# Edge stage of a two-layer graph network: ScalarE seeds the accumulators and takes the second LayerNorm's squares, attributes scaled before they are turned, GpSimd's DMAs in pairs

## The reference

```python
h = max(layernorm(x), 0)
m = concat(h[dst], h[src]) @ W_pre.T + b_pre            # one message per edge
mx, mn, s1, s2 = segment max, min, sum of m, sum of m*m  by dst      # deg = edges per node
std = sqrt(relu(s2/deg - (s1/deg)**2) + 1e-5)
agg = concat(mx, mn, s1/deg, std)                       # 0 for mx, mn, mean without an edge
scaled = concat(agg, agg * log(deg+1), agg / log(deg+1))
x = x + (concat(h, scaled) @ W_post.T + b_post) @ W_lin.T + b_lin
h = max(layernorm(x), 0)
a = segment_sum(edge_attr, dst) / max(deg, 1)
x = x + relu(concat(h, a) @ W1 + b1) @ W2 + b2
```

## Time and profile before

| what | value |
|---|---|
| median of 3 runs | 1627.22 us (1627.15 to 1629.86) |
| profiled execution | 1626.46 us, its span 1624.7 us |
| granted TensorE clock, mean | 0.973 of full |
| PE, DVE, ACT, POOL busy | 92%, 86%, 58%, 76% |
| DMA moved | 197.95 MB |

### The profile page before, as it was taken

The page is one execution under the profiler, slowest core; times in us unless marked ns, Lnnn a source line. Parts: engine busy times, 40 slices in busy tenths (PEclk is TensorE's granted clock), DMA queues, the critical chain, the costliest instruction groups (busy, mean ns, idle before and its releaser), DMA issues.

```text
span 1624.7 us, 33700 instructions
## 1 busy us (share of the span) xinstructions
PE 1494.9 (92%) x8747; PEld 1257.4 (77%) x8747; DVE 1397.1 (86%) x4327; ACT 939.8 (58%) x1976; POOL 1236.0 (76%) x1376
## 2 busy tenths in 40 slices
PE   2899999999999759999999999999998999999995
PEld 2799998889999648888777787777777777777783
DVE  5899999999999468899888997988887888888892
ACT  1799999999999534455444453434444444444341
POOL 1778777777778777888888888888888888888833
PEclk9899999999999979999999999999999999999997
DMA  3455555555555622233233333333332323333200
GB/s 88 163 209 206 207 207 201 201 201 204 204 203 206 187 87 85 84 86 90 90 91 92 93 92 91 92 91 89 93 91 79 95 86 89 94 93 93 89 18 15
DMA packets 158898, 197.95 MB, mean 122 GB/s; under 512 B 18912, under 2 KB 115321, under 8 KB 158858
## 3 DMA queue, kind: packets, MB, share of 16 engines
q1 hardware_dynamic: 136906, 149.93, 28.3%
q0 software_dynamic: 21952, 47.55, 9.5%
HBM read 111.11 MB, written 90.17 MB: 124 GB/s over the span
## 4 chain that ended last, share of the span: by engine, by line
PE 82%; DVE 6%; issue 5%; ACT 3%; another core or an unknown queue 3%; DMA 1%; SPq 1%; POOL 0%; DVEq 0%; ACTq 0%; POOLq 0%
PE bank L572 12%; PE bank L621 6%; PE bank L581 6%; PE bank L614 5%; PE bank L691 5%; PE bank L618 5%; PE bank L615 5%; PE bank L624 5%; PE bank L704 5%; PE bank L670 3%; PE bank L593 3%; PE bank L591 3%; PE bank L592 3%; PE bank L555 3%
## 5 line engine op out<-in xcount | busy, mean ns | idle before, releaser
L444 POOL DMA_INDIRECT rows<-table,idx x196 | 208.3, 1063 | 59.7 <-issue 59.7
L450 POOL DMA_INDIRECT y<-nout,oidx x196 | 200.0, 1020 | 70.6 <-issue 70.3
L444 POOL DMA_INDIRECT hs<-table,idx x196 | 204.8, 1045 | 44.7 <-issue 31.2
L614 PE MATMUL bank<-comb_lo,agg_hi 128*128 128x384 f32 x588 | 212.4, 361 | 16.6 <-DVE nout L1019 10.7
L572 PE MATMUL bank<-w_sb,nut 128*128 128x128 f32 x1568 | 202.9, 283 | 5.5 <-issue 4.7
L379 POOL TENSOR_TENSOR runs<-nx,b_all 128x512 f32<-128x512 f32 x98 | 125.9, 1284 | 107.9 <-DVE nx L1029 107.8
L572 PEld LDWEIGHTS bank<-w_sb,nut 128*128 128x128 f32 x1568 | 184.5, 193 | 23.1 <-issue 14.2
L618 PE MATMUL bank<-comb_hi,agg_lo 128*128 128x384 f32 x588 | 200.1, 340 | 0.0
L615 PE MATMUL bank<-comb_hi,agg_hi 128*128 128x384 f32 x588 | 199.5, 339 | 0.0
L781 ACT ACTIVATE nh<-nx,nms,nrs 128x128 f32<-128x128 f32 x392 | 161.8, 484 | 1.1 <-DVE nms L1002 0.5
L621 PE MATMUL bank<-comb_sd,agg_sd 128*128 128x384 f32 x392 | 159.6, 489 | 0.0
(11 more groups left out here) (180 smaller groups left out, 4196.9 us busy)
## 6 DMA issues: line engine op xcount, KB each, us to landing
table<-rows SPq DMA_DIRECT2D x98, 512.0 KB, 2.7
rows<-in_x SPq DMA_DIRECT2D x98, 256.0 KB, 3.1
y<-nout SPq DMA_DIRECT2D x98, 256.0 KB
inv<-inv_row SPq DMA_DIRECT2D x49, 256.0 KB
attr<-in_edge_attr SPq DMA_DIRECT2D x48, 256.0 KB
keep<-keep_row SPq DMA_DIRECT2D x49, 128.0 KB
reset<-reset_row SPq DMA_DIRECT2D x49, 128.0 KB
lift<-lift_row SPq DMA_DIRECT2D x49, 128.0 KB
```

What stands on the lines that cost most here:

```text
L444: pool.indirect_dma_start(out=to[:, s, j, :], out_offset=None, in_=of, in_offset=bass.IndirectOffsetOnAxis(ap=idx[:, s, which, j:j + 1], a ...
L450: pool.indirect_dma_start(out=out, out_offset=bass.IndirectOffsetOnAxis(ap=oidx[:, c % 4, j:j + 1], axis=0), in_=eout[:, c % 2, j, :], in_ ...
L614: pe.matmul(acc[:, 0:SCALERS * P], hi, w_lo, start=(a == MX), stop=False, skip_group_check=True)
```

## The change

It touches the edge stage and what is prepared for it.

- *Accumulators.* `layer0` no longer begins a sum; ScalarE writes the constant part (b_post, b_lin and now b_pre through the weights, `acc_seed`, 128x384) into the bank first (`seed`, in place of PE's wait for mix), and the matmuls add to it. Two matmuls `open_sums` come once. With b_pre there, `message` goes: the scans read PE's bank, 3 and 4 in turn, and mix takes `xd` as gathered, so `receiver_const` goes too.
- *b2* is written into bank 7 by ScalarE (`out_bias`) and not by a matmul.
- *Second LayerNorm.* The last mix operation gives the row sum (`accum_out`), DVE makes the negative mean from it, ScalarE the sum of squares with four ACTIVATEs (`squares`).
- *Attributes.* ScalarE multiplies each attribute row by 1/count before it is turned (`scale_attr`), and the scan's mask becomes `keepm` = (count-1)/count in F32, a fifth mask row of 256 KB per chunk; `run_attr` is the mean itself, and `mean_attr` goes.
- *GpSimd* gathers three chunks ahead and not four, with `pause` between pairs of DMAs; three factors are copied, two chunks ahead.
- *Orders* of PE, ScalarE and DVE within a step are new.

```diff
@@ GpSimd @@
-            def mean_attr(c, i):
-                ...
-                pool.tensor_tensor(attr_mean[:, c % 2, :], run_attr[:, c % 2, :], inv[:, c % 4, :],
-                                   ALU.mult).then_inc(sem("e_attr_mean"), 1)
+            def pause(n, c, i):
+                pool.tensor_tensor(pause_go[:, n:n + 1], eps_col[:], eps_col[:], ALU.add).then_inc(sem(f"e_paused{n}"), 1)
+                pool.wait_ge(sem(f"e_paused{n}"), c + 1 + EU * i)
+                go(3 + n)
...
             def edge_step(k, i):
-                if edge(k + 1):
-                    copy_scales(k + 1, i)
...
+                if edge(k + 3):
+                    gather_rows_of(k + 3, i)
...
-                if edge(k):
-                    mean_attr(k, i)
...
@@ PE @@
             def layer0(c, j, i):
-                if j >= 2:
-                    pe.wait_ge(sem("e_mixed"), TILES * c + j - 1 + TILES * EU * i)
-                elif c >= 1:
-                    pe.wait_ge(sem("e_mixed"), TILES * (c - 1) + j + 3 + TILES * EU * i)
+                pe.wait_ge(sem("e_seeded"), TILES * c + j + 1 + TILES * EU * i)
...
             def outputs(c, i):
-                pe.matmul(bank[7][:], ones[:], b2_rows[:], start=True, stop=False, skip_group_check=True)
+                pe.wait_ge(sem("e_b2"), c + 1 + EU * i)
...
@@ ScalarE @@
+            def squares(c, i):
+                ...
+                for j in range(TILES):
+                    last = act.activation(off2[:, j, :], x1[:, b, j, :], ACT.Square, bias=neg2[:, b, j:j + 1],
+                                          accum_out=sq2[:, b, j:j + 1])
...
-            def message(c, i):
-                ...
-                act.activation(bank[4][:], bank[3][:], ACT.Identity, bias=b_pre_col[:]).then_inc(sem("e_b"), 1)
...
+            def seed(c, j, i):
+                if c == 0 and j < 2:
+                    act.wait_ge(sem("e_sums_open"), 1)
+                elif j >= 2:
+                    act.wait_ge(sem("e_mixed"), TILES * c + j - 1 + TILES * EU * i)
+                else:
+                    act.wait_ge(sem("e_mixed"), TILES * (c - 1) + j + 3 + TILES * EU * i)
+                act.activation(bank[5 + j % 2][:, 0:SCALERS * P], acc_seed[:], ACT.Copy).then_inc(sem("e_seeded"), 1)
+
+            def scale_attr(c, i):
+                ...
+                act.wait_ge(sem("e_factors"), c + 1 + EU * i)
+                for j in range(TILES):
+                    last = act.activation(attr[:, c % 2, j, :], attr[:, c % 2, j, :], ACT.Copy,
+                                          scale=factor[:, c % 4, 2, j:j + 1])
...
             def edge_step(k, i):
...
                 if behind:
                     hidden(0, 7, k - 1, i)
+                if have:
+                    seed(k, 3, i)
...
@@ DVE, mix_plain @@
-                dve.tensor_tensor(x1[:, c % 2, j, :], acc[:, 0:P], part2[:, j % 2, :], ALU.add).then_inc(sem("e_mixed"), 1)
+                dve.scalar_tensor_tensor(x1[:, c % 2, j, :], acc[:, 0:P], 1.0, part2[:, j % 2, :], ALU.mult, ALU.add,
+                                         accum_out=sum2[:, c % 2, j:j + 1]).then_inc(sem("e_mixed"), 1)
```

More of the change, by code:

```diff
@@ L653, in turn_attr @@
             def turn_attr(c, i):
[L654 to L655 removed]
+                pe.wait_ge(sem("e_attr_scaled"), c + 1 + EU * i)
                 if c == 0:
@@ L676, in turn_normed @@
                     pe.wait_ge(sem("e_h2l"), c + EU * i)
+                if not last:
+                    pe.wait_ge(sem("e_hst"), c + 3 + EU * i)
                 for j in range(TILES):
@@ L714, in edge_step @@
                     layer0(k, 0, i)
-                if ahead:
-                    sender_part(k + 1, i)
-                    turn_receiver(k + 1, i)
-                if have:
                     layer0(k, 1, i)
@@ L875, in edge_step @@
             def edge_step(k, i):
-                ahead, behind = edge(k + 1), edge(k - 1)
+                have, ahead, behind = edge(k), edge(k + 1), edge(k - 1)
+                if k == 0:
+                    seed(0, 0, i)
                 if ahead:
                     sender_turned(k + 1, i)
+                if have:
+                    seed(k, 1, i)
                 if behind:
+                    squares(k - 1, i)
                     spread(k - 1, i)
-                if ahead:
-                    message(k + 1, i)
-                    receiver_turned(k + 1, i)
-                if behind:
-                    normalise(k - 1, i)
                 if ahead:
@@ L1278, in edge_step @@
                     scan_squares(k + 1, i)
+                    low_part(ME, mean_b[:], k + 1, i)
                     square_mean(k + 1, i)
[L1280 to L1285 removed]
                 if have:
@@ L1288, in edge_step @@
                 if ahead:
-                    low_part(ME, mean_b[:], k + 1, i)
+                    variance(k + 1, i)
+                    scan_max(k + 1, i)
                 if have:
                     mix(k, 3, i)
-                    moments(k, i)
+                if ahead:
+                    low_part(MN, run_min[:, (k + 1) % 2, :], k + 1, i)
+                if have:
+                    negative_mean(k, i)
+                if ahead:
+                    low_part(MX, run_max[:, (k + 1) % 2, :], k + 1, i)
             run_passes(dve, node_step, edge_step, first_step=-1)
```

304 lines of the change are left out of this document (165 added, 139 removed).

## The result

The changed kernel takes 1519.7 us (median of 4 runs, 1518.8 to 1522.4) against 1628.5 of the kernel before beside it: ratio 0.9334, 95% interval 0.9318 to 0.9351. The forecast was 1569 with a range of 1540 to 1606: the direction was right, the size too small by 49 us, and the case that came was the rival "PE becomes the bound", faster than I had it.

The account below looks back on a forecast made before the run. GpSimd was taken to bound the kernel before and after. Profiled 1626.5 us, less 56.6 (TensorE's step 47 at 1502.5 against 1559.1), plus 1 for the tail: 1570.9; median +0.8, start -3: 1569, range 1540 to 1606.

Parts of the forecast that it names:

- PE becomes the bound: Rival, edge stage: GpSimd's step falls under 19.5 us and TensorE sets the pace; 1556 us, or 1541; chance 0.28.
- What bounds before: Edge stage before the change: GpSimd, never waiting, sets the pace at 20.48 to 21.19 us a step; TensorE alone needs 19.16.
- GpSimd's step after, 18.0 us without stretch: GpSimd's edge step after the change: its operations sum to 18.0 us, 1.1 below before, with 1.4 of pauses paid back.
- With 7.8 to 11.3% it becomes 19.5 to 20.3 us. I take 19.9: GpSimd's edge step: DVE's two-input operations lengthen its 18.0 us by that share, so GpSimd still decides.
- PE 19.1 us a step: TensorE's edge step after the change: 19.1 us, between 18.75 without a stall and 19.5.
- the matmul of b2, taken as 0.4: TensorE's edge step: leaving out this matmul takes 0.4 us off 19.16, giving 18.75 without a wait.
- the two stalls of 0.1 to 0.2 each: TensorE's edge step: waits for `hst` at `sender_part` (0.1 to 0.2 us) and for seed 3 (0 to 0.2).
- The start, -3: First three edge steps: 3 us less, as TensorE loses the b2 matmul and the wait for GpSimd's last operation.
- ScalarE, DVE, SP hidden, seeds at 0.5: Edge step: ScalarE about 15 us and DVE some 17 stay under TensorE, SP's extra mask row costs nothing, seeds 0.5 each.
- the two ScalarE rivals: Late releases in ScalarE's queue: 1.1 us a step, 1605 us, chance 0.14; or 2.2 every step, 1653, within slower's 0.10.
- The rival of dear pauses: GpSimd's pauses cost 0.7 us each, not 0.27: step 21.8 us with stretch, 1651 us; within slower's chance of 0.10.
- the tail's +1: End of the kernel: squares on ScalarE in the last norm and one pause add 1 us.

## Why the prediction missed

1. *What bounds before* was right: GpSimd, to the step. The experiments show it: 84 us from 1.1 us a step less on GpSimd, nothing from 0.62 less on TensorE.
2. *GpSimd's step after, 18.0 us without stretch*: right within 0.15; 18.15 by the run in which nothing stretches it.
3. *"With 7.8 to 11.3% it becomes 19.5 to 20.3 us. I take 19.9"* is the step that failed. The stretch is no share of the work. An operation is lengthened where it starts while DVE reads two SBUF tensors; where GpSimd's step lies against DVE's decides how many do, and how long. In the changed kernel with work added, where GpSimd is slower than TensorE, the lag wanders between 1 and 6.5 us and the stretch costs 1.4 to 1.65 us. Where its step without stretch lies under TensorE's, by as little as 0.27 us, the lag becomes constant and the stretch is only what fills the room: 18.56 in place of 19.9. I had a GpSimd that sets the pace before me, and carried its price to one that follows. That it settles is seen in the lags; why it does, and why at that place, is argued and not shown apart. By 19.9 GpSimd held TensorE for half the steps, so TensorE's step 47 stood at 1502.5; with TensorE alone it is 1488.3: 14.2 of the 47.6 us by which step 47 came sooner.
   I gave little to the one page that spoke against this. The Trainium skill, SBUF — State Buffer, section "Who interferes with whom", says that such a DVE operation contends with GpSimd's reads of SBUF and that the order of issue decides who waits. By that rule the first table above is what one expects of the small operations, and the trace agrees: 0.20 us alone, 0.63 on the mean where DVE comes first. It agrees for DVE too: 21 of the 26 long DVE operations start after the 128x512 operation of GpSimd beside them (the other five shortly before it). I had read the lengthened gathers as evidence against it and did not ask when each had started, which the earlier trace rows already told. Its inference that descriptor work is not held is only half borne out: a DMA that starts inside is longer by 0.07 to 0.29 us on the mean, one that DVE overtakes is not.
4. *PE 19.1 us a step* is the other step that failed, and the larger in time: 18.56, 23.6 us over 44 steps. Two terms were mis-sized: the matmul of b2, taken as 0.4, is worth 0.62, and the two stalls of 0.1 to 0.2 each do not occur (the step is that of the kernel before without b2 and with GpSimd relieved, 18.54, where no seed is waited for). `hst` and seed 3 are in time, seed 3 by 0.13 us: the layout by hand was right on where it is tight, and erred by 0.1 to 0.3 us at each place.
5. *The start, -3*, an estimate outside the sum for step 47: measured 9.8. The receiver constant is what it hangs on, since cutting that alone gains 13.9 us by step 3. How 1.1 us of it a step become 13.9 is not shown: with it cut, DVE's first `mix` waits for it until 583.11 us; with it whole, PE's first tile waits until 587.01 for the last outputs of the node stage. The changed kernel gives 4 of the 13.9 back, 3.4 by its pauses (without them step 3 begins at 634.7), of which 1.2 show in the medians.
6. *ScalarE, DVE, SP hidden, seeds at 0.5*: right; their work is less than I had (13.6 us a step for 15 on ScalarE, 15.7 for 17 on DVE). Squares are at 0.39, with 0.19 for reading the sum that lies beside the next one. No release of ScalarE was late in the changed kernel's profile, and the two ScalarE rivals fell. The rival of dear pauses fell too: they cost GpSimd the 1.4 us that I had worked out.

14.2 + 23.6 + 9.8 = 47.6, the miss of step 47 (1502.5 forecast, 1454.9 measured); and the tail's +1 did not come. The direction was forecast for the right reason, relief of GpSimd. The size was not.

## What to carry to other kernels

When the engine that sets the pace is relieved, ask first which engine is next, and price that one without waits from a stretch of the trace in which it had none. A contention that depends on who starts first is no percentage: here it cost 1.4 to 1.65 us a step where the lengthened engine set the pace, and nothing where that engine had 0.27 us of room or more. An instruction on an engine that waits costs nothing, and the same instruction can cost more than its bar once that engine is the bound: here 0 and 29 us.

## What the runs showed of the hardware

- A GpSimd DMA issue or tiny operation that starts while DVE runs an operation with two SBUF inputs is lengthened (in the kernel before from 0.98 to 1.27 us on the mean for a DMA, from 0.20 to 0.63 for a tiny operation); a DMA that DVE overtakes is not (0.97 to 0.98).
- DVE's two-input operations are lengthened by GpSimd's 128x512 operations: 26 of 218 from 0.68 to over 0.9 us in the kernel before, up to 2.45, and none of 246 where GpSimd has no such operation.
- GpSimd kept a lag behind TensorE of 7.56 to 7.68 us over 36 steps in the changed kernel, with no wait beyond its usual gaps of 0.3 and 0.57 us. That the lengthening alone holds it there is argued, not shown.
- A 128x512 operation of GpSimd took 1.06 us where both inputs were one tensor, and 1.29 where they were two.
- Reading the sum of an `accum_out`: 0.19 us on ScalarE and 0.08 on DVE, mostly beside the next operation.
